# AdaLN conv-and-linear kernel: layer 0's demodulation scales in two halves, its first bias product behind stage two

## The reference, cut to what matters

```python
def _layer(x, style, w, b, mw, mb, typ):          # four of them in a row, per layer
    s = style @ mw.T + mb                          # one style per sample (64) and input channel (64)
    weight = SCALE * w * s[:, None, :, None]
    demod = lax.rsqrt(jnp.sum(weight * weight, axis=(2, 3)) + EPS)
    weight = weight * demod[:, :, None, None]
    ...                                            # conv 'same', 'upsample' + blur, 'same', blur + 'downsample'; + b
x = x + cond0(x) @ identity.T                      # layer 0: 64 samples of 64 x 1024
x = x + linear1(cond1(x))                          # layer 1: linear 1024 x 1024, plus rank-8 experts with gates
```

## Time and profile before

| | |
|---|---|
| Median of 3 runs | 1484.4 us (1483.89 to 1484.7) |
| Profiled execution, its own time | 1485.3 us |
| Its span in the trace | 1483.5 us |
| PE busy | 1457.1 us (98%) |
| DVE / ACT / POOL busy | 993.6 (67%) / 720.3 (49%) / 461.4 us (31%) |
| Granted TensorE clock, mean | 0.999 of full speed |

### The profile page before, as it was taken

One profiled execution on the slowest core, in us unless ns is written; L12 is line 12 of the kernel. 1 busy time (PEld: TensorE's weight loads), 2 busy tenths in 40 slices (PEclk: granted clock), 3 DMA queues, 4 the chain that ended last, 5 costly groups with the idle time before them and its releaser, 6 DMA issues.

```text
span 1483.5 us, 28219 instructions
## 1 busy us (share of the span) xinstructions
PE 1457.1 (98%) x9619; PEld 1370.7 (92%) x9619; DVE 993.6 (67%) x2361; ACT 720.3 (49%) x1618; POOL 461.4 (31%) x536
## 2 busy tenths in 40 slices
PE   5999999999999999999989999999999999999999
PEld 4889899989988988888879999999999999999998
DVE  7766567765566656555676677677677677677674
ACT  4455455545544544455444454454454454454452
POOL 3133233323323332333313233233233232232230
PEclk9999999999999999999999999999999999999999
DMA  5343423443343244324533424424424324324322
GB/s 121 110 104 94 115 85 88 118 116 88 84 114 98 74 114 113 97 73 113 142 114 86 112 61 110 111 59 113 111 58 113 108 61 113 107 62 113 107 63 71
DMA packets 56635, 145.14 MB, mean 98 GB/s; under 512 B 19365, under 2 KB 21861, under 8 KB 56586
## 3 DMA queue, kind: packets, MB, share of 16 engines
q1 hardware_dynamic: 55928, 144.19, 36.2%
q10 hardware_dynamic: 658, 0.30, 0.1%
HBM read 110.92 MB, written 33.55 MB: 97 GB/s over the span
## 4 chain that ended last, share of the span: by engine, by line
PE 95%; DVE 3%; DMA 0%; issue 0%; ACT 0%; SPq 0%; POOL 0%; DVEq 0%; POOLq 0%; ACTq 0%
PE bank L1552 48%; PE bank L1404 13%; PE bank L1406 13%; PE bank L1405 13%; PE bank L1712 4%; PE bank L1584 1%; PE bank L1573 1%; PE bank L1617 1%; PE bank L1646 0%; DMA ends<-in_x_dram 0%; DVE win L1142 0%; PE bank L1729 0%; PE bank L1635 0%; DVE fw_l L1136 0%; DVE mtmp L1141 0%
## 5 line engine op out<-in xcount | busy, mean ns | idle before, releaser
L1552 PE MATMUL bank<-fw_h,ct_h 128*128 128x354 f32 (+2 forms) x1256 | 448.2, 357 | 0.8 <-DVE xout L1107 0.8
L1552 PE MATMUL bank<-fw_l,ct_h 128*128 128x354 f32 (+2 forms) x1256 | 444.7, 354 | 0.0
L1552 PE MATMUL bank<-fw_h,ct_l 128*128 128x354 f32 (+2 forms) x1256 | 442.9, 353 | 0.0
L414 POOL COPY conv_buf<-edge 128x4 f32 (+1 forms) x128 | 21.2, 193 | 849.6 <-DVE tw L1238 835.8
L1552 PEld LDWEIGHTS bank<-fw_h,ct_l 128*128 128x128 f32 x1256 | 236.1, 188 | 21.3
L1552 PEld LDWEIGHTS bank<-fw_h,ct_h 128*128 128x128 f32 x1256 | 236.6, 188 | 17.6 <-DVE ct_l L1262 0.9
L1552 PEld LDWEIGHTS bank<-fw_l,ct_h 128*128 128x128 f32 x1256 | 236.5, 188 | 15.5
L405 POOL TENSOR_TENSOR d_l<-d_f,d_h 128x512 fp32r<-128x512 f32 x128 | 154.7, 1208 | 104.5 <-ACT d_h L617 104.3
L1404 PE MATMUL bank<-d_h,tw 128*128 128x256 f32 x640 | 181.5, 284 | 0.3 <-DVE beta L957 0.3
L1406 PE MATMUL bank<-d_h,tw 128*128 128x256 f32 x640 | 180.6, 282 | 0.0
L1405 PE MATMUL bank<-d_l,tw 128*128 128x256 f32 x640 | 180.3, 282 | 0.0
(11 more groups left out here) (244 smaller groups left out, 3113.2 us busy)
## 6 DMA issues: line engine op xcount, KB each, us to landing
xraw<-in_x_dram SPq DMA_DIRECT2D x32, 512.0 KB, 6.6
xres<-in_x_dram SPq DMA_DIRECT2D x32, 512.0 KB, 4.1
x_dram<-xout SPq DMA_DIRECT2D x32, 512.0 KB, 2.9
xraw<-x_dram SPq DMA_DIRECT2D x32, 512.0 KB, 6.5
xres<-x_dram SPq DMA_DIRECT2D x32, 512.0 KB, 4.6
xraw<-in_x_dram SPq DMA_DIRECT2D x32, 511.5 KB, 8.0
xraw<-x_dram SPq DMA_DIRECT2D x32, 511.5 KB, 7.9
out_dram<-xout SPq DMA_DIRECT2D x31, 512.0 KB, 2.9
```

The source lines that it names most:

```text
L1552: last = mm(ffn_ps[e][:, 0:cols.stop - cols.start], ctf((ct_h, ct_h, ct_l)[part], k), (fw_h, fw_l, fw_h)[part][:, k, cols], start=k == beg ...
```

## The change

The roots are taken for a range of convolutions: first for convolutions 2 and 3 (counted from 0), which `lam3` needs (through convolution 2), then for 0 and 1. `lam3` is made between the two. VectorE's `v_low(0)` moves from behind the tables to behind the second reciprocal. TensorE does stage u before it waits for the tables, and its bias product 0 and the first half of `ends_2` come behind stage u, with bias product 1 behind these. ScalarE waits for the tables (`scales_made` 2) before `z_high(0)`, because stage u no longer stands behind them.

```diff
--- before.py
+++ after.py
@@ -701,6 +701,7 @@
                     x_high(ly, 0, 0)
                     x_high(ly, 0, 1)
                     prep_m4(ly, (0, 1))
+                    act.wait_ge(zs["scales_made"], 2)
                     z_high(0)
                     t_high(0)
                     act.wait_ge(s["bias_ready"], 3)
@@ -829,19 +830,19 @@
                 v.tensor_scalar(dvar[:, :, :], bank[6][:, 0:NL * NB].rearrange("p (l b) -> p l b", l=NL),
                                 SCALE * SCALE, EPS, ALU.mult, ALU.add).then_inc(s["dvar_ready"], 1)
 
-            def prep_roots(ly, link):
+            def prep_roots(ly, link, ls=slice(0, NL)):
                 dve.wait_ge(ly["s"]["dsqrt"], 1)
-                link(v.reciprocal(dsq, dsq))
-
-            def prep_roots_2(ly, link):
-                dtmp = ly["scratch"]
-                link(v.tensor_tensor(dtmp[:, :, :], dsq, dsq, ALU.mult))
-                link(v.tensor_tensor(dtmp[:, :, :], dtmp[:, :, :], dvar[:, :, :], ALU.mult))
-
-            def prep_roots_3(ly, link):
-                dtmp = ly["scratch"]
-                link(v.tensor_scalar(dtmp[:, :, :], dtmp[:, :, :], -0.5, 1.5, ALU.mult, ALU.add))
-                link(v.tensor_tensor(d_all[:, :, :], dtmp[:, :, :], dsq, ALU.mult))
+                link(v.reciprocal(dsq[:, ls, :], dsq[:, ls, :]))
+
+            def prep_roots_2(ly, link, ls=slice(0, NL)):
+                dtmp = ly["scratch"][:, ls, :]
+                link(v.tensor_tensor(dtmp, dsq[:, ls, :], dsq[:, ls, :], ALU.mult))
+                link(v.tensor_tensor(dtmp, dtmp, dvar[:, ls, :], ALU.mult))
+
+            def prep_roots_3(ly, link, ls=slice(0, NL)):
+                dtmp = ly["scratch"][:, ls, :]
+                link(v.tensor_scalar(dtmp, dtmp, -0.5, 1.5, ALU.mult, ALU.add))
+                link(v.tensor_tensor(d_all[:, ls, :], dtmp, dsq[:, ls, :], ALU.mult))
 
             def prep_lam2(ly):
                 stt(out=ly["lam2"][:, 0:NB], in0=ly["s_all"][:, 1, :], scalar=SCALE, in1=ly["s_all"][:, 2, :],
@@ -1301,15 +1302,18 @@
                     prep_scales(ly)
                     prep_down(ly, link)
                     opening_down(link)
-                    prep_roots(ly, link)
-                    prep_roots_2(ly, link)
-                    prep_roots_3(ly, link)
+                    prep_roots(ly, link, slice(2, 4))
+                    prep_roots_2(ly, link, slice(2, 4))
+                    prep_roots_3(ly, link, slice(2, 4))
                     prep_lam3(ly).then_inc(zs["scales_made"], 1)
+                    prep_roots(ly, link, slice(0, 2))
+                    v_low(0)
+                    prep_roots_2(ly, link, slice(0, 2))
+                    prep_roots_3(ly, link, slice(0, 2))
                     prep_tables(ly, link)
                     prep_tables_2(ly)
                     prep_tables_3(ly, link)
                     dve.sem_inc(zs["scales_made"], 1)
-                    v_low(0)
                     prep_bias(ly, link, 0)
                     ends_1()
                     z_low(0)
@@ -1737,12 +1741,12 @@
                     stage_v(0)
                     turn_weights(0, 2)
                     ends_1()
+                    pe.wait_ge(s["split_ready"], 2)
+                    stage_u(0)
                     pe.wait_ge(zs["scales_made"], 2)
                     prep_bias(ly, 0)
-                    pe.wait_ge(s["split_ready"], 2)
-                    stage_u(0)
+                    ends_2(range(2))
                     prep_bias(ly, 1)
-                    ends_2(range(2))
                     pe.wait_ge(s["split_ready"], 3)
                     stage_t(0)
                     ends_2(range(2, 4))
```

## The result

The changed kernel takes **1490.28 us** (median of 6 runs, 1489.33 to 1492.07) against 1484.48 (1483.89 to 1485.36) for the kernel before, measured beside it: a ratio of 1.0036, 95% interval 1.0025 to 1.0046. A later set gave 1490.38 against 1485.68, again 1.0036 (1.0023 to 1.0050). The change makes the kernel slower by about 5 us. The forecast was 1489.3, with a range of 1487.0 to 1491.0.

What follows compares the result with a forecast made beforehand. The prediction took VectorE to bound the opening, its instructions blocked by GpSimd's. t_low 5.5 us later less 0.6 back gives 4.9, so 1483.5 becomes a 1490.2 execution and a 1489.3 us median; range 1487.0 to 1491.0.

Steps and rivals of the forecast that it cites:

- Step 1: VectorE up to lam3: with half the reciprocal first, lam3 ends at 26.7 instead of 27.70, 1.0 us earlier.
- Step 2: Stage u: starts at 28.5 instead of 30.13, v_high beside the second reciprocal; the 0.41 us wait ahead of z_f goes.
- Step 3: Tables: four VectorE instructions each wait for a GpSimd subtraction, so scales_made 2 comes at 34.3 instead of 29.1.
- near-tie: At the tables: GpSimd's d_l starts at 28.6, as the second of the second half's four Newton instructions is issued.
- Step 4: Up to z_f: VectorE stands 0.9 us for bias product 0; z_f starts at 37.4 instead of 32.98, 4.4 us later.
- Step 5: TensorE behind z_f: half of ends_2 and bias product 1 at 1.2 GHz put t_low at 42.2, 5.5 us later.
- Step 6: Behind t_low: the next pair's d_f starts earlier and meets both L1142, giving 0.6 us back, between nothing and 1.2.
- The sum: Opening: 5.5 − 0.6 = 4.9 us later, taken over whole by TensorE's dense work.
- (a): Tables: port stays with VectorE or GpSimd comes later; z_f only 1.1 late, 1484.9 to 1486.5 us; chance 0.13.
- (b): Tables: several VectorE instructions pass per GpSimd gap, saving 1.5 to 3 us; 1486.5 to 1488.0 us; chance 0.12.
- (c): Opening faster: stage u ends 2.9 us earlier and GpSimd waits throughout; 1483.9 us; chance 0.03.
- (d): Clock stays at 1.2 GHz through stage t into the convolution, 3.8 us more; 1490.6 to 1493 us; chance 0.07.

Runs made afterwards that it cites:

- e1: Changed kernel with GpSimd's four subtractions (d_l, o_l, twice) held until the tables are done: 1488.99 us, ratio 1.0022.
- e8: Changed kernel with 24 unread products of 256 columns behind stage u and 12 behind bias product 0, keeping TensorE busy: 1488.20 us, ratio 1.0014.
- e2: Changed kernel with bias product 1 ahead of the first half of ends_2 on TensorE: 1489.24 us, ratio 1.0024.
- e3: Kernel before with only the roots split in two halves around lam3, every other order as it was: 1489.73 us, ratio 1.0028.
- e4: Changed kernel with the roots whole again, keeping only the new order (v_low behind lam3, then the tables): 1490.29 us, ratio 1.0035.
- e6: Changed kernel with both GpSimd's subtractions held behind the tables and bias product 1 ahead of ends_2: 1486.64 us, ratio 1.0006.
- e9: Changed kernel with subtractions held behind the tables, bias product 1 first, unread filler products (24 and 12) and both d_f holds: 1486.94 us, ratio 1.0011.
- e7: Kernel before with the next pair's d_f held until VectorE's ends_2 is done and the first pair's until down is made: 1483.96 us, ratio 0.9984.
- e10: e7 with 28 products that nothing reads behind ends_1 in TensorE's idle time: 1484.32 us, ratio 0.9992 to the kernel before.

## Why the prediction was right

| step | forecast | first profile | second profile |
|---|---|---|---|
| `lam3` ends | 26.7 | 25.28 | 26.38 |
| `v_l` starts | 27.6 | 26.18 | 27.28 |
| stage u starts | 28.5 | 27.07 | 28.17 |
| last table ends | 34.3 | 32.50 | 33.60 |
| `z_f` starts | 37.4 | 35.98 | 37.07 |
| L957, second time | 40.6 | 39.78 | 40.78 |
| `t_low` starts | 42.2 | 41.38 | 42.38 |
| time | 1489.3 | 1490.28 (median) | 1490.38 (median) |

**Step 1** held in size where the load lands as in the earlier trace rows: 1.3 us earlier against 1.0. What I left out is that the landing differs from execution to execution: `d_f` started at 20.64 and at 19.47 in two profiles of one kernel. It moves the block from L880 to the Newton steps and `lam3` by 1.1 us.

**Step 2** held: the second reciprocal covers `v_high`, and stage u was done 3.9 us ahead of the tables, at the higher clock.

**Step 3** was the right mechanism, 0.4 us too long: 7.2 us and not 7.6. Four instructions wait for four subtractions, as said, but the near-tie went the other way. L840 slipped in ahead of `d_l`, and L844, L845, L859 and L861 were the four. e1 shows 3.0 us of it to be the block: 7.22 became 4.27.

**Step 4** was 0.4 short. Bias product 0 exposed 1.27 us and not 0.9, because it ran at 1.2 GHz itself: 1.12 us and not 0.66. With the clock up (e8) it exposed 0.81. I had applied the low clock only to what comes behind it.

**Step 5** had the right mechanism, by e8 and e2, but was 0.5 to 0.6 us short: `z_f` to `t_low` took 5.40 and 5.31 us, where the forecast has 4.8 (42.2 − 37.4). From the start of `ends_2`'s half to the second L957 took 4.14 us, against 2.56 + 0.92 = 3.48. The four products of `ends_2` had 2.73 us up to the next start, and the 0.92, read between two starts, leaves out that VectorE must wait for the last product to end: 1.41 us from the first record of bias product 1 to L957.

**Step 6** held: `t_low` to `ends_3` gave 0.8 us back against 0.6 (41.38 − 36.68 = 4.70 became 53.74 − 49.83 = 3.91). `d_f` met both L1143 and cost them 1.0 us together (1.20 and 1.05 for 0.65), where it had cost L1142 and L1179 1.8.

**The sum** for the opening, 4.9, was 3.9 in the first profile and 4.9 in the second. That it hits in the second is partly luck: steps 1 and 3 came out 0.3 and 0.4 lower than forecast, steps 4 and 5 0.4 and 0.5 higher. The first profile's span grew by 5.0 all the same: the clock fell once more at 781 us, at the change of layers, as the stretch from 781 to 782 shows, where the kernel before kept it; its opening's 3.9 became 5.2 there. In the second profile it did not, and the span grew by 4.7. The median came out 1.0 above the forecast. The term missing from the sum is most likely this further fall. Profiles with one such fall have a mean clock of 0.995 (the first of the changed kernel, e3, e4, e6), those with the 10.2 us of the opening alone 0.996 or 0.997 (the second, e1, e2). Nine of the changed kernel's eleven executions had 0.994 or 0.995, so by this estimate nine had a further fall; in four profiles it cost 1.2 to 2.2 us. What brings it was not settled. That the clock is low for 10 us of the opening goes with TensorE's idle times there: in e8, where filler took these up, it did not fall.

Of the **rivals**, (a) is out by the changed kernel's own rows and e1's, and (b) by e4's. Against (c), e9's median with every repair lies 1.2 us above the kernel before, which has none, though part of that is the filler's. (d) did not happen in the two profiles, where the clock was back at 40.4 and 40.5, during stage t.

## What to carry to other kernels

Before a chain on VectorE is moved or lengthened, look at what GpSimd does beside it. A VectorE instruction with all its operands in SBUF, a reciprocal or memset excepted, can be held until GpSimd's is done, and a chain that just fits ahead of GpSimd's start pays once it no longer does: here 0.5 to 0.9 us for each of four instructions, 3.0 us in all. Giving a stage its input earlier also starts everything else that hangs on that input. And where TensorE idles ahead of a product, that product may run at half clock (here 1.12 us instead of 0.66), so a short product that another engine waits for is best issued ahead of a long one.

## What the runs showed of the hardware

- The turn at the port is one for one in these rows, also for VectorE instructions issued back to back without a semaphore (e4: 1.16, 0.91, 1.22 and 0.88 us for instructions of 0.2). Three kinds ran at their free times beside GpSimd, as e7 shows: the reciprocal (1.74 us beside `d_f`), an instruction with a PSUM input (L1143, 0.68 beside `o_l`) and a memset (0.27 beside `d_l`). The Trainium skill (SBUF — State Buffer, SBUF: two separate sides) tells of an exclusive lock held for a whole instruction, which these ends bear out; the turn-taking is shown by these rows alone.
- GpSimd pays too: `d_l` took 1.33 and 1.22 us instead of 1.18 where short VectorE instructions came between, and the second `d_l` of the kernel before took 1.63, since L1142 (0.70 us) had started 0.1 us ahead of it.
- The kernel's own scatter goes with the clock. Of the kernel before, 24 executions with a mean clock of 0.999 had a median of 1484.7 us, and 19 with 0.997 one of 1486.4, on one chip.
- Products that nothing reads held the clock up in the opening (e8, e9), and cost their overrun where the work that was waited for stood behind them: 1.1 us in e9, 0.7 in e10. In e10 the clock fell later, at 41 us.
